# Gated cross-attention block with a quantised FFN: projections ahead of biases, entry 1 through another bank, the last entry's FFN on VectorE, and unread products in TensorE's waits

## The reference, cut to what matters

```python
x = x + tanh(g_xattn) * xattn(layernorm(x), ctx, mask, mask, Wq, bq, Wk, bk, Wv, bv)
x = x + tanh(g_ffn)   * ffn(layernorm(x), W1, W2)
# xattn: q = Wq xn + bq, k = Wk ctx + bk, v = Wv ctx + bv; 16 heads of 8 channels,
#        softmax over 256 source positions with both masks, out = heads side by side
# ffn:   act_quant(y) @ weight_quant(W1).T -> silu -> act_quant(h) @ weight_quant(W2).T
# act_quant: rows scaled by 127 / max|row| and rounded; weight_quant: -1, 0, 1 times mean|w|
```

## Time and profile before

| | |
|---|---|
| median of 3 runs | 226.73 us (226.59 to 228.67) |
| profiled execution | 227.11 us, of it the span 225.6 us |
| busy: TensorE, VectorE, ScalarE, GpSimd | 176.1, 135.4, 119.2, 93.1 us |
| granted clock, mean | 0.929 |
| the chain that ended last | TensorE 50%, VectorE 19%, GpSimd 11%, ScalarE 8%, issue 6%, DMA 4% |

### The profile page before, as it was taken

One profiled execution on the slowest core, in us unless ns is written; L12 is line 12 of the kernel. 1 busy time (PEld: TensorE's weight loads), 2 busy tenths in 40 slices (PEclk: granted clock), 3 DMA queues, 4 the chain that ended last, 5 costly groups with the idle time before them and its releaser, 6 DMA issues.

```text
span 225.6 us, 4985 instructions
## 1 busy us (share of the span) xinstructions
PE 176.1 (78%) x1922; PEld 101.0 (45%) x1934; DVE 135.4 (60%) x264; ACT 119.2 (53%) x167; POOL 93.1 (41%) x165
## 2 busy tenths in 40 slices
PE   1578589889896997897999969979988899953513
PEld 0445434355464453554555435546554555522111
DVE  2457924656875693679686846887785635171310
ACT  2325134887977756463665555646645574721301
POOL 8634893200356227203853480057008204617250
PEclk9999857999999999999999999999999999995555
DMA  5484651200000022000010230000000000000000
GB/s 144 90 266 155 201 209 40 53 6 4 0 6 17 4 47 51 0 4 0 4 17 17 47 87 23 4 0 4 23 4 1 21 8 3 0 23 4 25 0 23
DMA packets 8055, 9.23 MB, mean 41 GB/s; under 512 B 1420, under 2 KB 6732, under 8 KB 8028
## 3 DMA queue, kind: packets, MB, share of 16 engines
q1 hardware_dynamic: 7080, 8.45, 13.3%
q10 hardware_dynamic: 952, 0.46, 0.8%
HBM read 5.66 MB, written 1.05 MB: 30 GB/s over the span
## 4 chain that ended last, share of the span: by engine, by line
PE 50%; DVE 19%; POOL 11%; ACT 8%; issue 6%; DMA 4%; POOLq 1%; ACTq 0%; DVEq 0%
PE ps_exp L932 22%; PE ps_pv L948 8%; DVE nmx L699 7%; ACT probs L536 4%; PE ps_max L1010 3%; PE ps_exp L994 3%; DVE hb L746 2%; PE ps_max L925 2%; DVE hs L751 2%; POOL y L382 2%; DMA brow<-in_L_xattn_bq 2%; POOL hq L409 2%; PE ps_exp L822 2%; ACT hb L585 2%; DMA q<-negm 2%
## 5 line engine op out<-in xcount | busy, mean ns | idle before, releaser
L699 DVE TENSOR_REDUCE nmx<-ps_max 128x2 f32<-128x512 f32 x122 | 78.3, 684 | 35.2 <-PE ps_max L925 34.9
L536 ACT ACTIVATE probs<-ps_exp 128x1024 f32<-128x1024 f32 x64 | 65.5, 1023 | 52.7 <-PE ps_exp L932 52.3
L932 PE MATMUL ps_exp<-q,k 32*128 32x256 f32 x512 | 74.7, 409 | 17.3 <-DVE nmx L699 13.0
L925 PE MATMUL ps_max<-k,q 32*128 32x256 f32 x488 | 71.4, 410 | 0.6 <-DVE q L641 0.4
L932 PEld LDWEIGHTS ps_exp<-q,k 32*128 32x128 f32 x512 | 46.7, 189 | 39.8 <-issue 24.3
L925 PEld LDWEIGHTS ps_max<-k,q 32*128 32x128 f32 x488 | 43.2, 190 | 1.2 <-issue 0.8
L948 PE MATMUL ps_pv<-probs,v_aug 128*32 128x256 f32 x512 | 41.3, 395 | 0.0
L403 POOL TENSOR_SCALAR hs<-hs,ys 128x1 f32<-128x1 f32 x8 | 3.0, 375 | 59.8 <-DVE hs L751 59.8
L948 PEld LDWEIGHTS ps_pv<-probs,v_aug 128*32 128x32 f32 x512 | 10.1, 108 | 21.4 <-issue 21.0
L746 DVE SCALAR_TENSOR_TENSOR hb<-hb,ps_exp 128x512 f32<-128x512 f32 x16 | 11.0, 686 | 12.7 <-ACT hb L585 12.7
L376 POOL TENSOR_TENSOR qk<-qk,mask_b 128x512 f32<-128x512 f32 (+1 forms) x8 | 9.1, 1137 | 18.7 <-ACT qk L501 18.7
(11 more groups left out here) (133 smaller groups left out, 230.2 us busy)
## 6 DMA issues: line engine op xcount, KB each, us to landing
w_nat<-in_L_ffn_W SPq DMA_DIRECT2D x2, 1024.0 KB, 6.9
out<-x_sb SPq DMA_DIRECT2D x8, 128.0 KB, 1.7
c_sb<-in_ctx SPq DMA_DIRECT2D x3, 256.0 KB, 8.8
mask_b<-in_mask_Bx1x_fk SPq DMA_DIRECT2D x1, 768.0 KB, 7.7
k<-qk SPq DMA_DIRECT2D x12, 64.0 KB
q<-qk SPq DMA_DIRECT2D x12, 64.0 KB
x_sb<-in_x SPq DMA_DIRECT2D x1, 512.0 KB, 8.6
x_sb<-in_x SPq DMA_DIRECT2D x2, 128.0 KB, 3.3
```

The costliest lines, as they stand in the source:

```text
L536: nc.scalar.activation(probs[:, s % PROBS, :], ps_exp[:, exp_at[("exp", s)] % 2, :], ACT.Exp).then_inc(S["exp_done"], 1)
L699: nc.vector.tensor_reduce(max_columns(g, hh), ps_max[:, at % VEC, :].rearrange("t (c s) -> t c s", c=DC), AX_X, ALU.max, negate=True).then ...
L925: return nc.tensor.matmul(bank[:, c * T:(c + 1) * T], at_rows(q4, b, h)[:, c * 128:(c + 1) * 128], at_rows(k4, b, h), start=True, stop=True)
L932: return nc.tensor.matmul(bank[:, o:o + T], at_rows(k4, b, h)[:, c * 128:(c + 1) * 128], at_rows(q4, b, h), start=True, stop=True)
```

## The change

The step tables are rewritten: entry 1's projections leave `ps_exp` and step -6 and go in step -5 through `ps_pv` (event `second`); `first3`, `turn_v`, the first `v` and `clear` move later; in each entry from `y_max` on the events move one or two steps later; the last entry has its own table, with its events ahead of those of the entry before it in the same step. TensorE projects u = 0 and then u = 1 around the turning of the biases. `clear_rows(0)` on GpSimd comes after both inverse deviations, and the load of Wq moves to SyncE's queue. In the last entry VectorE normalises, takes the largest and rounds y (`last_y`) and scales h (`last_h`); h is rounded in halves by VectorE and GpSimd and its turned halves are copied by ScalarE and VectorE. Products of the identity with itself, which nothing reads (`keep_busy`), stand in five places of TensorE's stream.

```diff
-        FIRST_EVENTS = {"first2": -7, "k": -6, "q": -6, "first3": -5, "rows_k": -5, "rows_q": -5, "turn_v": -4, "copy_v": -4,
-                        "mrow": -4, "load_w": -4, "v": -3, "clear": -2}
+        FIRST_EVENTS = {"first2": -7, "second": -5, "first3": -3, "rows_k": -4, "rows_q": -4, "turn_v": -2, "copy_v": -2,
+                        "mrow": -2, "load_w": -4, "v": -1, "clear": 1}
-        ENTRY_EVENTS = {"att": 10, "back": 11, "y_max": 13, "y_quant": 13, "y_turn": 15, "upa": 16, "ha": 16, "ra": 17,
-                        "upb": 18, "hb": 18, "rb": 19, "h_quant": 19, "h_turn": 21, "down": 23}
+        ENTRY_EVENTS = {"att": 10, "back": 11, "y_max": 14, "y_quant": 14, "y_turn": 16, "upa": 17, "ha": 17, "ra": 18,
+                        "upb": 19, "hb": 19, "rb": 20, "h_quant": 20, "h_turn": 23, "down": 25}
+
+        LAST_EVENTS = {"att": 10, "back": 11, "y_max": 12, "y_turn": 12, "upa": 15, "ha": 15, "ra": 15, "upb": 15, "hb": 15,
+                       "rb": 15, "h_quant": 15, "h_turn": 18, "down": 19}
-        LAST = HP * (B - 1) + 24
+        LAST = HP * (B - 1) + 20
...
+            return use + [(w, b) for b in reversed(range(B)) for w, at in (LAST_EVENTS if b == B - 1 else ENTRY_EVENTS).items()
+                          if s == HP * b + at]
...
             sp.dma_start(wqkv[:, 1, :], Wk).then_inc(S["ld_wk"], 16)
+            sp.dma_start(wqkv[:, 0, :], Wq).then_inc(S["ld_wq"], 16)
...
-            clear_rows(0)
             for i in range(2):
                 entry_std(i)
-            pool.wait_ge(S["xn_first"], 2)
+                pool.wait_ge(S["xn_first"], i + 1)
+            clear_rows(0)
             identity(ident16)
...
+            def quantise_h_last():
+                pool.wait_ge(S["hq_last"], 1)
+                pool.wait_ge(S["exp_full"], exp_at[("h_turn", B - 2)] + 1)
+                nc.gpsimd.tensor_scalar(hq[:, 512:1024], hb[:, 512:1024], hs[:, B - 1, 3:4], ROUND, ALU.mult, ALU.add).then_inc(S["hq_last_b"], 1)
...
+            def evac_second(what):
+                o = "qk".index(what)
+                act.wait_ge(S["first_ready"], FIRST_ORDER.index(("q", "second")) + 1)
+                nc.scalar.activation(qk[:, o, T:2 * T], first_bank(what, "second"), ACT.Identity,
+                                     bias=biases[:, 2 * QH + 1 - o:2 * QH + 2 - o]).then_inc(S["first_bias"], 1)
...
             turn_k()
+            normalise_first(0)
             entry_stats(1)
-            normalise_first(0)
+            normalise_first(1)
             dve.wait_ge(S["bias_full"], 1)
...
-            normalise_first(1)
...
+            def last_y():
+
+                b = B - 1
+                at = [ys[:, b, i:i + 1] for i in range(4)]
+                dve.wait_ge(S["ln2_stats"], B)
+                dve.wait_ge(S["std_last"], 1)
+                dve.wait_ge(S["yq_ready"], B - 1)
+                link(nc.vector.tensor_scalar(y[:], x_sb[:, b, :], mv2[:, 0:1], rstd2[:], ALU.subtract, ALU.mult))
+                link(nc.vector.tensor_reduce(at[0], y[:], AX_X, ALU.max, apply_absolute_value=True))
+                link(nc.vector.tensor_scalar(at[1], at[0], 1e-5, 1.0 / 127.0, ALU.max, ALU.mult))
+                link(nc.vector.reciprocal(at[2], at[1]))
+                dve.wait_ge(S["exp_full"], exp_at[("y_turn", b - 1)] + 1)
+                nc.vector.tensor_scalar(yq[:], y[:], at[2], ROUND, ALU.mult, ALU.add).then_inc(S["yq_last"], 1)
+                nc.vector.tensor_scalar(at[3], at[1], half_mean[:], None, ALU.mult).then_inc(S["ys_last"], 1)
+
+            def last_h():
...
+                dve.wait_ge(S["h_max"], 2 * B)
...
+                nc.vector.tensor_scalar(hq[:, 0:512], hb[:, 0:512], at[3], ROUND, ALU.mult, ALU.add).then_inc(S["hq_last"], 1)
...
+            def last_h_turned():
...
+                nc.vector.tensor_scalar(hT[:, 512:1024], src, -ROUND, None, ALU.add).then_inc(S["hT_last_b"], 1)
...
+            def keep_busy(n, bank):
+
+                for i in range(n):
+                    nc.tensor.matmul(bank[:, 0:128], ident[:], ident[:], start=True, stop=True)
+
+            def project_second():
+
+                pe.wait_ge(S["first_bias"], 2)
+                pe.wait_ge(S["ld_ce"], 16)
+                pe.wait_ge(S["std_T"], 2)
+                pe.wait_ge(S["xn_first"], 2)
+                nc.tensor.matmul(first_bank("k", "second"), wT[:, 1, :], c_sb[:, 0, T:2 * T], start=True, stop=True).then_inc(S["first_ready"], 1)
+                nc.tensor.matmul(first_bank("q", "second"), wT[:, 0, :], xn[:, T:2 * T], start=True, stop=True).then_inc(S["first_ready"], 1)
+
             pe.wait_ge(S["consts"], 2)
+            keep_busy(10, ps_max[:, 2, :])
             turn_projection("k", "ld_wk")
             turn_projection("q", "ld_wq")
+            keep_busy(3, ps_max[:, 2, :])
+            pe.wait_ge(ld_c[0], 16)
+            project_first("k", 0)
+            project_first("q", 0)
             pe.wait_ge(S["ld_bias"], 32)
             nc.tensor.transpose(bias_bank, brow[:], ident[0:2 * QH, 0:2 * QH]).then_inc(S["bias_full"], 1)
-            pe.wait_ge(ld_c[0], 16)
-            for what, u in FIRST_ORDER[0:4]:
-                project_first(what, u)
+            project_first("k", 1)
+            project_first("q", 1)
...
                     if what == "back":
+                        if i == B - 1:
+                            keep_busy(6, ps_pv)
                         turn_back(i)
                     if what == "y_turn":
+                        if i == B - 1:
+                            keep_busy(12, ps_pv)
                         turn_y(i)
...
                     if what == "h_turn":
+                        if i == B - 1:
+                            keep_busy(16, ps_pv)
                         turn_h(i)
```

More of the change, by code:

```diff
@@ L373, in mask_qk @@
                     pool.wait_ge(S["ld_mask_rest"] if p else S["ld_mask1"], 16)
-                pool.wait_ge(S["mix_out"], mix_at[(what, p)] + 1)
+                if p:
+                    pool.wait_ge(S["mix_out"], mix_at[(what, p)] + 1)
+                else:
+                    pool.wait_ge(S["first_bias"], FIRST_ORDER.index((what, "second")) - 3)
                 at, b0 = columns(p), 2 * p + 1 - (p > 0)
@@ L416, in _ @@
                         mask_first("q", int(what[-1]))
+                    if what == "second":
+                        mask_qk("k", 0)
+                        mask_qk("q", 0)
                     if what == "clear":
@@ L547, in _ @@
                         evac_first("q", int(what[-1]))
+                    if what == "second":
+                        evac_second("k")
+                        evac_second("q")
                     if what == "turn_v":
@@ L588, in _ @@
                             act.wait_ge(S["vec_full"], vec_at[("down", i - 1)] + 1)
-                        nc.scalar.activation(hT[:], bank[:, 0:512].bitcast(F16), ACT.Copy, bias=-ROUND).then_inc(S["mix_out"], 1)
+                        at = slice(0, 512 if i == B - 1 else 1024)
+                        nc.scalar.activation(hT[:, at], bank[:, 0:512].bitcast(F16)[:, at], ACT.Copy, bias=-ROUND).then_inc(S["mix_out"], 1)
         @block.vector
@@ new lines, in last_h @@
+            def last_h():
+                b = B - 1
+                at = [hs[:, b, i:i + 1] for i in range(6)]
+                step = ys[:, b, 3:4]
+                dve.wait_ge(S["h_max"], 2 * B)
+                dve.wait_ge(S["ys_last"], 1)
+                link(nc.vector.tensor_scalar(at[1], at[0], at[5], step, ALU.max, ALU.mult))
+                link(nc.vector.tensor_scalar(at[1], at[1], 1e-5, None, ALU.max))
+                link(nc.vector.reciprocal(at[2], at[1]))
+                nc.vector.tensor_scalar(at[3], at[2], step, 127.0, ALU.mult, ALU.mult).then_inc(S["hq_last"], 1)
+                dve.wait_ge(S["hq_last"], 1)
+                dve.wait_ge(S["exp_full"], exp_at[("h_turn", b - 1)] + 1)
+                nc.vector.tensor_scalar(hq[:, 0:512], hb[:, 0:512], at[3], ROUND, ALU.mult, ALU.add).then_inc(S["hq_last"], 1)
+                link(nc.vector.tensor_scalar(at[4], at[1], gate_mean[:], None, ALU.mult))
@@ L787, in _ @@
                     if what == "y_max":
-                        y_max(i)
+                        if i < B - 1:
+                            y_max(i)
+                        else:
+                            last_y()
+                    if (what, i) == ("h_quant", B - 1):
+                        last_h()
+                    if (what, i) == ("h_turn", B - 1):
+                        last_h_turned()
                     if what == "ha":
@@ L810, in project @@
                         pe.wait_ge(S["ld_ce"], 16)
-                if what in "kq" and p == 0:
-                    pe.wait_ge(S["std_T"], 2 - o)
-                if what == "q" and p == 0:
-                    pe.wait_ge(S["xn_first"], 2)
                 if what == "v" and p == 0:
@@ L999, in turn_h @@
                 bank = take_exp(("h_turn", b))
-                pe.wait_ge(S["hq_ready"], b + 1)
```

(12 more changed lines are left out.)

58 lines of the change are left out of this document (37 added, 21 removed).

## The result

The changed kernel takes 225.14 us (median of 20 runs, 223.44 to 227.53) against 226.96 (226.03 to 230.05) for the kernel before in the same runs: ratio 0.990 [0.987, 0.992], faster by 1.0%. The forecast was 2.4%, and 221.4 us. The direction was right, less than half of the size came. One caution: the ratios are formed from the executions in the fast state alone and the medians from all, and the profiled executions of the changed kernel (227.51 us, span 225.2) and of experiment 2 (226.61 us) were slow ones. The profile of experiment 5, whose code is the same up to the last turn of h, is therefore shown beside that of the changed kernel where the start is measured.

What follows compares the result with a forecast made beforehand. It saw chains of waits as the bound: biases then four serial projections at the start, VectorE's idling before y's largest, engines taking turns in the tail. Terms summed to -5.4 us, giving 221.4 us; range 217.3 to 225.2.

Steps and rivals of the forecast that it cites:

- the start: Up to the first exponential's scores: reordered projections and earlier maxima bring scores at 22.0 to 22.1 instead of 25.13, -3.0 us.
- rival 2: Start gives little: SyncE's later loads or the shift's DMA behind them hold steps 0 and 1; 223.9 us, chance 0.17.
- The clock behind it: After about 26 us: TensorE's clock falls again, but half of the low stretch's cost is taken back, -1.5 us.
- The second weight's turn: Step 16: with y's turn one step later, ScalarE's copies no longer hold the scores until 70.67, -1.25 us.
- The steady steps: Loop: waits for y and h's rounding go, the shared step grows by 1.5; -0.9 us, between -4 and +3.
- Rival 3: Slower: the shared step grows by 1.5 in seven entries and relieved steps give nothing back; 228.1 us, chance 0.07.
- Steps 56 to 63: Last steps of the loop: they gain entry 4's down product and lose the others, +0.5 us.
- The tail: After the last exponential: sixteen unread products delay h's turn, end at 28.8 against 28.1, +0.7 us.
- rival 1: Tail: the sixteen products are no obstacle, tail -2.4 in place of +0.7; 218.3 us, chance 0.22.
- The halves: Last entry's h rounding: VectorE's and GpSimd's halves run one behind the other, 0.5 us more, hidden behind unread products.
- The sum: Whole kernel: the forecast's terms together give -5.4 us and a median of 221.4 us.

Runs made afterwards that it cites:

- experiment 2: Changed kernel with `clear_rows(0)` back ahead of the inverse deviations on GpSimd: 221.28 us, 0.972 of the kernel before.
- experiment 5: Changed kernel without the sixteen unread products ahead of the last turn of h: 220.80 us, 0.969 of the kernel before.
- experiment 7: Changed kernel with the old step table and order for entries 0 to 5: 228.11 us, 1.002 of the kernel before.
- experiment 1: Changed kernel with SyncE's large loads sent ahead of the constant rows that wait for `clear_rows`: 223.09 us, 0.971 of the kernel before.
- experiment 3: Changed kernel with 1 MB of x and ctx loads sent behind entry 1's copies, with the FFN weights: 221.94 us, 0.973 of the kernel before.
- experiment 6: Changed kernel with large loads ahead of the constants and without sixteen unread products before h's last turn: 217.96 us, 0.955 of the kernel before.
- experiment 9: As experiment 6, also without the 6 and 12 unread products ahead of the last entry's turns: 217.19 us, 0.954 of the kernel before.
- experiment 4: As experiment 1, also without the 10 and 3 unread products at the start: 225.32 us, 0.977 of the kernel before.

## Why the prediction was right and wrong, by its steps

**The step that failed is the start: "copied at 18.9, issued at 19.0. Before, from the issue at 22.07 to the scores at 25.13 it took 3.1 us. So scores at 22.0 to 22.1: -3.0 us".** Everything up to the issue was right (unit 0's maxima at 11.85 for 11.4, issue at 19.03 for 19.0, warm projections 0.44 us apart, 7.42 and 7.86, for 0.43). The 3.1 us were taken over into a stretch with other traffic. They became 8.8 in the changed kernel's profile, 7.2 in that of experiment 5 and 5.8 in that of experiment 7: scores at 27.83, 25.57 and 24.62, a change of +2.7, +0.4 and -0.5 us in place of -3.0. The clock that fell during the wait then held back the first exponential by another 0.9 us, so that it started 3.7, 1.3 and 0.5 us behind the kernel before.

The same part noted that SyncE's queue runs about four us later, and rival 2 named the very mechanism, "the shift's small DMA behind the large ones". What I did not do was price it: I gave it a lead of 0.5 us, and a chance of 0.17, without adding up which bytes would be in flight at 19 us. The loads before were issued from 9 to 12 us and their traffic had ended by 20 (share 0.16 and 0.14 in the two windows to 24); issued four us later, they reach to 24 by that alone, by this estimate. The FFN weights, issued at 22.5, follow them; experiment 7 shows 5.8 us without them, and what they add to the rest is not separated. Experiments 1, 2 and 3 each take the bytes away by another means, and in each the scores come 3.5 to 4.3 us behind the issue and no longer wait for the store. That is shown.

**The clock behind it: -1.5.** Steps 0 to 15 gave 0.9 (0.4 in the profile of experiment 5), but the reason was not the one given. The low stretch did not shorten: it ran from 23.7 to 37.4 us, 13.7 us, against 10.2 before (26.2 to 36.4), and 10.2 in experiment 5 (25.7 to 35.9). TensorE had stood idle ahead of the fall in the first and the last of these. The wait alone does not set the length: in experiment 2, where it is gone, the low stretch is again 13.7 us (19.7 to 33.4), experiment 1 has 3.4 us, and experiment 6, with the same start as 1, has none up to 46 us. Which part of the 0.9 is clock and which is order, and what decides the length, stays open.

**The second weight's turn: -1.25.** Right, -1.38 in the step from 15 to 16.

**The steady steps: -0.9.** Right in sign, too small: -2.3 between steps 16 and 56, of a bound of -4. (The 2.7 us of experiment 7 also hold the second weight's turn and steps 56 to 63.) Step lengths of steps 32 to 47 (first the entry whose steps also project k and q, then one without), from start to start of the exponentials:

```
before   2.26 3.31 3.02 2.96 2.17 3.32 3.19 2.74 | 2.26 2.26 3.02 2.96 2.17 3.31 2.05 2.75
after    2.26 4.61 2.69 3.59 2.05 2.25 2.06 2.29 | 2.26 3.66 2.89 2.87 2.18 2.86 2.05 2.30
```

The shared step grew by 1.3 and 1.4 (3.31 to 4.61, 2.26 to 3.66; forecast 1.5 each). In the entry with k and q the waits for h's rounding and for y went: 3.32 to 2.25 and 3.19 to 2.06, 1.1 each, as priced. The rest, the relief of the other steps, I had at 1.15 a pair (3.0 - 2.2 - 1.15 = -0.35, which is 43.4 for 43.75); it is 1.4 net (down's old step alone gives 0.45 in each entry, h's turn 0.45 in the entry without k, while the step that now has up b takes 0.63 more in the entry with k, 2.96 to 3.59). So two of the three terms were off by 0.2 to 0.3, both one way, and their sum, -0.35 a pair, became -0.9 (42.87) and in the first pair -1.3 (42.42): a small difference of large terms. Rival 3, relieved steps that give nothing back, did not happen.

**Steps 56 to 63: +0.5.** They gave +0.8.

**The tail: +0.7.** Right in mechanism: tanh of entry 7 at 14.4 us behind the last exponential (forecast 14.8), entry 6's products at the low clock, h rounded at 19.9 (19.8), and then the unread products, 5.46 us (5 to 6), the turn 5.2 us behind the rounding, the end at 27.8 (28.8). The size was 1.0 too high, so the tail came out 0.3 us shorter than before instead of 0.7 longer: the products started at 19.8 (20.1) and held the turn for 5.3 us (5.9). Experiment 5 gives 4.2 us back by taking them out; rival 1 is refuted.

**The halves.** GpSimd's half of 512 columns took 0.98 us beside VectorE's 0.49, while a whole row of 1024 takes it 1.12 alone (L427): more than 0.4 us longer than half of that. The rule of the Trainium skill ("SBUF — State Buffer", SBUF: two separate sides), that GpSimd and certain VectorE instructions hold one port pair in turn, agrees with this. An estimate: VectorE's half starts at 213.74, and its 0.49 us and half of the 1.12 behind it end at 214.79; GpSimd's half ended at 214.78. The forecast of some 0.5 us more was right. It was hidden behind the unread products, as expected; I had it come out where they are gone, and in experiment 5 it doesn't show either: the turn starts at 212.85 as entry 6's down product runs out (211.20 and 1.87 long), and GpSimd's half ends at 212.96.

**The sum.** The terms add up to -5.45, and 221.3 us for the 221.4 given, which changes nothing. With the start of experiment 5, start and clock missed by 5.4 us together, and the other stages came out 2.3 us better than forecast (the loop by 1.4, the tail by 1.0), which nobody had priced: that the total missed by no more than 3.1 us is in part luck.

## What to carry to other kernels

A latency measured in one stretch belongs to the traffic of that stretch: when work on a queue moves, add up the bytes that will be in flight at the moment at which a small, critical DMA is issued, on whichever queue, and send the large loads first or later. Moving an idle engine's work out of the way can delay a second queue that waits for it, and the delay shows up ten us later. Unread products that keep the clock up can pay ahead of work whose operand isn't there yet (at the start here), buy nothing where another wait stands behind them (experiment 9), and cost their time ahead of a turn that is ready: here 1.3 us bought for 5.2. And one profile is one execution: the same start showed its first exponential at 26.75, 27.60 and 29.95, so look for a second profile of the same code before sizing a term by it.

## What the runs showed of the hardware that I had not expected

- A small store of 8 KB needed at most 3.1 to 4.3 us from issue to its reader where the windows behind its issue show a DMA share of 0.14 to 0.7 (before, experiments 1, 2 and 3), 5.8 us where they show 0.9 for its first three us and then 0.4 (experiment 7), and 7.2 and 8.8 us where they show 0.9 and more nearly throughout (experiment 5, changed kernel).
- Thirteen unread products at the start held back the first turn of a weight from 3.85 (experiment 4) to 6.18 (experiment 1), and yet the first exponential came 1.0 to 3.0 us earlier with them.
- The first stretch at the low clock behind 18 us was 3.4 us long in experiment 1, 10.2 before and in experiment 5, 13.7 in the changed kernel and experiment 2, and 17.1 in experiment 7; the runs do not show what decides it.
- An unread product of two records took 0.24 us at 2.4 GHz (24 records in 2.84 us) and 0.34 in the last place, where the clock rose on the way (32 records in 5.46).
